# Three seams of a two-part attention kernel: matmuls in pairs, loads and norms moved ahead, a last step in banks of its own

## What is computed

```
x = x + dense_attention(layernorm(x))          # 16 heads of 64, causal penalty -50, softmax over 512
y = layernorm(x)
for i in range(6):
    y = local_attention(shift_tokens(y), Wqkv[i], q_scale[i], k_scale[i], Wo[i]) + y
    #   q, k: divided by their norm per head, times a scale, rotary tables; windows of 32 that
    #   look at themselves and at the window before
    y = ffn(shift_tokens(y), ln_g[i], ln_b[i], W1[i], b1[i], W2[i], b2[i]) + y
    #   layernorm; (a * gelu(gate)) @ W2 + b2, inner width 341
out = x + y
# shift_tokens: of each token the upper 64 channels are those of the token before
```

## Time and profile before

| | us |
|---|---|
| median of 3 runs (lowest to highest) | 2168.26 (2166.22 to 2171.08) |
| the profiled execution: its own time | 2178.13 |
| its span, first to last instruction | 2176.4 |
| PE busy | 2060.6 (95%) |
| DVE busy | 1491.7 (69%) |
| POOL busy | 1451.8 (67%) |
| ACT busy | 1317.8 (61%) |
| DMA queue q1, share of 16 engines | 36.5% |
| mean granted TensorE clock, share of full | 0.976 |

### The profile page before, as it was taken

The page is one execution under the profiler, slowest core; times in us unless marked ns, Lnnn a source line. Parts: engine busy times, 40 slices in busy tenths (PEclk is TensorE's granted clock), DMA queues, the critical chain, the costliest instruction groups (busy, mean ns, idle before and its releaser), DMA issues. The chain is left out here.

```text
span 2176.4 us, 61276 instructions
## 1 busy us (share of the span) xinstructions
PE 2060.6 (95%) x23760; PEld 1286.0 (59%) x23760; DVE 1491.7 (69%) x3292; ACT 1317.8 (61%) x2522; POOL 1451.8 (67%) x1438
## 2 busy tenths in 40 slices
PE   8999999997589999999999999999999999999984
PEld 4555554553356566666666666666666666666652
DVE  5555565553677677777777777787777777777741
ACT  5666656654255566665666666666666666666651
POOL 3334443332677788888877888787887788778740
PEclk9999999998699999999999999999999999999996
DMA  2000000002245555455554564545544455444520
GB/s 64 6 1 6 1 1 6 1 1 71 75 109 132 131 138 127 106 131 148 133 126 104 133 169 111 126 112 134 158 118 118 116 148 142 117 117 122 125 60 22
DMA packets 217695, 204.95 MB, mean 94 GB/s; under 512 B 31682, under 2 KB 210880, under 8 KB 217408
## 3 DMA queue, kind: packets, MB, share of 16 engines
q1 hardware_dynamic: 217408, 201.04, 36.5%
HBM read 83.53 MB, written 13.63 MB: 45 GB/s over the span
## 5 line engine op out<-in xcount | busy, mean ns | idle before, releaser
L736 POOL TENSOR_TENSOR T<-T,RB 128x512 f32<-128x512 f32 x384 | 480.4, 1285 | 237.5 <-DMA RB<-norms 237.5
L684 POOL TENSOR_TENSOR T<-T 128x512 f32<-128x512 f32 x384 | 491.9, 1283 | 58.0 <-DVE T L679 57.6
L658 PE MATMUL bank<-XT,WQK 128*128 128x256 f32 x1536 | 404.2, 397 | 28.4 <-DVE T L679 19.6
L770 PE MATMUL bank<-WU,XT 128*32 128x512 f32 x3072 | 415.5, 601 | 1.5 <-ACT U L777 1.4
L413 POOL TENSOR_SCALAR PR<-PR,RI 128x512 f32<-128x512 f32 x256 | 173.9, 691 | 314.1 <-DVE RI L354 314.1
L664 ACT ACTIVATE SQ<-bank 128x512 f32<-128x512 f32 x384 | 224.6, 599 | 243.2 <-PE bank L658 242.9
L658 PEld LDWEIGHTS bank<-XT,WQK 128*128 128x128 f32 x1536 | 279.5, 194 | 151.2 <-issue 68.4
L678 DVE TENSOR_TENSOR T<-bank,TAB 128x512 f32<-128x512 f32 x384 | 261.9, 682 | 138.0 <-POOL T L684 64.2
L349 DVE CUSTOM_DVE_ANT_0 PR<-bank,causal 128x512 f32<-128x512 f32 x256 | 174.2, 681 | 201.1 <-PE bank L192 201.0
L777 ACT ACTIVATE U<-bank 128x512 f32<-128x512 f32 x384 | 228.7, 596 | 97.0 <-PE bank L770 96.4
L679 DVE TENSOR_TENSOR T<-bank,TAB 128x512 f32<-128x512 f32 x384 | 261.2, 680 | 0.0
(11 more groups left out here) (113 smaller groups left out, 3136.3 us busy)
## 6 DMA issues: line engine op xcount, KB each, us to landing
RB<-norms SPq DMA_DIRECT2D x384, 128.0 KB, 3.4
KZ<-T SPq DMA_DIRECT2D x384, 128.0 KB, 2.5
QP<-T SPq DMA_DIRECT2D x192, 256.0 KB, 4.8
TAB<-rotary_dram SPq DMA_DIRECT2D x24, 512.0 KB, 5.6
norms<-RN SPq DMA_DIRECT2D x96, 128.0 KB, 1.7
WQK<-wqk_halves_dram SPq DMA_DIRECT2D x12, 512.0 KB, 5.8
WVS<-wv_turned_dram SPq DMA_DIRECT2D x29, 128.0 KB, 3.4
WOS<-wo_lanes_dram SPq DMA_DIRECT2D x29, 128.0 KB, 3.6
```

Source lines behind the costliest of these rows:

```text
L658: m = pe.matmul(b[:, ab * HALF:(ab + 1) * HALF], WQK[n % 3][:, i, ab, :], XT[s % 2][:, hf * HALF:(hf + 1) * HALF], start=True, stop=True)
L684: pool.tensor_tensor(t1, t1, T2[i % 2][:, ::-1, :], ALU.add).then_inc(l_rotated.sem, 1)
L736: pool.tensor_tensor(t1, t1, RB[:, i:i + 1, :].to_broadcast([P, 2, HALF]), ALU.mult).then_inc(l_scaled.sem, 1)
L770: i = pe.matmul(bank[1][h * WIN:(h + 1) * WIN, :], XT[s % 2][:, c0:c0 + WIN], WU[:, lp * HG + h, :], start=True, stop=True)
```

## The change

There are four edits; the rest of both parts stays, instruction for instruction.

The core of the diff (left out: ACT's and DVE's new dense orders, which follow PE's, and the early norm's helpers, which are the old ones with other semaphores):

```diff
+        def load_first():
+            sp.dma_start(QSC[:, :], qsc).then_inc(s_i, 16)
+            for n in range(2):
+                load_weights(n)
+            for part in range(4):
+                load_table(part)
...
             def pe_project_q(u):
...
+                if u >= 2:
+                    pe.wait_ge(s_kkept, u + 1)
+                pe.matmul(bank[7 if u >= 2 else 6][:, :], W0[:, 0, p * P:(p + 1) * P], XNT[:, b * SEQ:(b + 1) * SEQ], start=True, stop=True).then_inc(s_q, 1)
...
             def pe_dense_program():
                 pe_ln_turn(0)
-                for g in range(-5, STEPS1 + TPB):
...
+                for h in range(-3, 2 * UNITS + 3):
+                    u, side = divmod(h, 2)
...
+                    if unit(u):
+                        pe_turn(2 * h)
...
+                    if side == 0 and unit(u + 1):
+                        pe_project_v(u + 1)
+                    if side == 1 and unit(u + 2) and not (vo or ln):
+                        pe_project_k(u + 2)
+                    if unit(u):
+                        pe_turn(2 * h + 1)
+                    if side == 0 and unit(u - 2) and u < UNITS:
+                        pe_project_out(u - 2)
...
+                    if unit(u - 1) and u != UNITS - 1:
+                        pe_values(u - 1, 2 * side)
+                        pe_values(u - 1, 2 * side + 1)
...
+                    if h != -2 and unit((h + 2) // 2):
+                        pe_scores(2 * h + 4)
+                        pe_scores(2 * h + 5)
...
+                    if g >= 90 and g % 4 == 2 and (g - 90) // 4 < 4:
...
+                        fold_scale(0, (g - 90) // 4).then_inc(s_fold, 1)
...
-                sp.dma_start(X2S[1:P, :, DH:E], xb[0:P - 1, :, DH:E]).then_inc(s_shift, 16)
+                for r0, r1 in ((0, 112), (112, P - 1)):
+                    sp.dma_start(X2S[r0 + 1:r1 + 1, :, DH:E], xb[r0:r1, :, DH:E]).then_inc(s_shift, 16)
...
+            def up_bank(s, i):
+                return bank[6] if s < LAST else bank[(0, 2, 3, 5, 1, 4)[i]]
...
+            def pe_last_down():
...
+                for c, (c0, n) in enumerate(FFR):
+                    pe.wait_ge(f_gated.sem, f_gated.at(LAST, c))
+                    for t in range(TPB):
+                        i = pe.matmul(bank[6][:, t * E:(t + 1) * E], GE[c][0:n, t * P:(t + 1) * P], W2S[0:n, c, :], start=c + t == 0, stop=c == len(FFR) - 1, skip_group_check=True)
+                i.then_inc(f_down_done.sem, 1)
...
             def act_layers_program():
                 act.preload_act_table_set('natural_log_exp_and_others')
-                for b in range(BATCH):
-                    r = slice(b * TPB, (b + 1) * TPB)
-                    act.activation(XM[:, r, :], X[:, r, :], ACT.Copy).then_inc(lxm.sem, 1)
+                r = slice((BATCH - 1) * TPB, BATCH * TPB)
+                act.activation(XM[:, r, :], X[:, r, :], ACT.Copy).then_inc(lxm.sem, 1)
...
             def pool_layers_program():
-                pool_ln2(0)
                 pool.wait_ge(s_i, 16 * NI)
-                for part in range(4):
-                    pool_fold_scale(0, part)
+                pool.sem_inc(l_folded.sem, 4)
                 for k in range(-8, TOTAL + 3):
                     pool_slot(k)
+                pool_ffn_norm(LAST)
                 pool_ffn_b2(LAST - 1)
-                pool_ffn_norm(LAST)
-                pool_ffn_b2(LAST)
+                pool_last_rest()
```

More of the change, by code:

```diff
@@ L87, in build @@
         s_k = keep.enter_context(nc.semaphore('s_k'))
+        HALF = SEQ // 2
+        WQK = [sb(f'WQK{i}', [P, HG, 2, P]) for i in range(3)]
+        TAB = sb('TAB', [P, 2, 2, 2, SEQ])
+        QSC = sb('QSC', [P, DEPTH * 4])
+        B1T = sb('B1T', [P, DEPTH * 6])
+        B2A = sb('B2A', [P, DEPTH, E])
+        GBA = sb('GBA', [P, 2, DEPTH])
+        s_i = keep.enter_context(nc.semaphore('s_i'))
+        s_wk = [keep.enter_context(nc.semaphore(f's_wk{i}')) for i in range(3)]
+        s_tb = [keep.enter_context(nc.semaphore(f's_tb{i}')) for i in range(4)]
+        NI = 5
         UNITS = BATCH * PAIRS
@@ L160, in pe_project_q @@
                 if u == 0:
[L161 to L167, removed]
                     pe.wait_ge(s_wqkv[1], 16)
-                if u >= 3:
-                    pe.wait_ge(s_res, u - 2)
+                if u >= 4:
+                    pe.wait_ge(s_res, u - 3)
                 else:
                     pe.wait_ge(s_vkept, u)
+                if (u - 2) % PAIRS == 3:
+                    pe.wait_ge(s_vok, u // PAIRS + 1)
+                if u % PAIRS == 7 and u < UNITS - 1:
+                    pe.wait_ge(s_xnt, b + 2)
                 pe.matmul(bank[7][:, :], W0[:, 1, p * P:(p + 1) * P], XNT[:, b * SEQ:(b + 1) * SEQ], start=True, stop=True).then_inc(s_kd, 1)
@@ new lines, in act_dense_program @@
+                for h in range(-3, 2 * UNITS + 3):
+                    u, side = divmod(h, 2)
+                    ahead = unit((h + 1) // 2)
+                    if ahead:
+                        act_exp(2 * h + 2, 0)
+                        act_exp(2 * h + 2, 1)
+                    if unit(u):
+                        act_keep_probs(2 * h)
+                    if side == 0 and unit(u + 1):
+                        act_keep_v(u + 1)
+                    if side == 1 and unit(u) and u % PAIRS == 3:
+                        act_first_vo(u // PAIRS)
+                    if side == 1 and 0 <= u < UNITS - PAIRS and u % PAIRS == 5:
+                        act_ln_keep(u // PAIRS + 1)
+                    if ahead:
+                        act_exp(2 * h + 3, 0)
+                    if unit(u):
+                        act_keep_probs(2 * h + 1)
+                    if ahead:
+                        act_exp(2 * h + 3, 1)
+                    if side == 0 and PAIRS <= u < UNITS and u % PAIRS == 4:
+                        act_early_keep(u // PAIRS - 1)
+                    if side == 1 and unit(u + 2):
+                        act_keep_q(u + 2)
+                    if side == 1 and unit(u - 1) and u != UNITS - 1:
+                        act_keep_values(u - 1)
+                    if h == 2 * UNITS - 2:
+                        act_keep_values(u - 1)
@@ L537, in build @@
             s_shift = ctx.enter_context(nc.semaphore('s_shift'))
-            NI = 5
             sigs = []
@@ L1305, in sp_layers_program @@
                 sp_shift(LAST)
+                for b in range(BATCH):
+                    sp_out(b)
+                sp.wait_ge(s_d, 16 * BATCH)
                 for i in range(3):
```

360 lines of the change are left out of this document (194 added, 166 removed).

## The result

Before and after ran side by side. The kernel after took 2103.39 us (median of 4 runs, 2099.16 to 2106.78), the kernel before 2169.67 us (4 runs, 2166.22 to 2172.57): a ratio of 0.9685, 95% interval 0.9667 to 0.9704. A later comparison on another chip gave 0.9666 (0.9653 to 0.9679). So the change takes 66 to 73 us off; the prediction was 71.5, to 2096.8 us.

A forecast was written before the change was run, and what follows sets the result against it. PE bounds the dense part; a loop through POOL, SP and DMA paces the layers. Terms -22 - 17 - 11 - 21.5 = -71.5 us from the 2168.3 median give 2096.8, own range 2083 to 2110, with rivals 2079 to 2119.

The forecast's parts named there:

- loop scale, relayout, RB: Layers: this loop through POOL, SP and DMA sets the pace, with PE having under 2% of slack.
- Edit 1: Dense part: paired score and value groups on PE save 0.74 us per unit; -22 us, bounds -24 to -12.
- the price of the projections: Dense part: projections cost 0.95 ahead of values and 0.89 ahead of a turn, saving about 0.10 us per unit for two.
- the part's end: End of the dense part: values and projection of the second last unit come later, 0.9 us set against edit 1.
- The rival that the copies of bank 7 hold PE up: Dense part: late ACT or bank 7 copies leave half units as long as before; edit 1 gives 0, 2119; chance 0.11.
- Edit 2: Seam: loads, folds and early norms moved into the dense part; -17 us, bounds -12 to -20.
- Edit 3: Shift split into 112 and 15 rows spreads over DMA engines: -11 us in the layers, -6 at the end.
- the term for the layers: Layers, edit 3: blocked issues ending after the scale go, 11.9 us together, taken as -11; bounds 0 to 20.7 and some.
- PE is the floor: Layers, rival: PE's own time caps the loop's gain, edit 3 gives 3 instead of 11, 2105; chance 0.10.
- Edit 4 with the end: Last step: six products back to back, with the shift's 6 us and some clock gain; -21.5 us, bounds -13 to -26.5.
- The 7.3 us of the working: Last step: full clock instead of half would save 7.3 us on products and down chunk; 2.2 was taken.

The follow-up runs named there:

- split_only: The kernel before with only the shift of 127 rows split into DMAs of 112 and 15 rows; 0.9941 of before, -12.8 us.
- proj_last: The kernel after with projections Q and out behind the values of their half unit instead of ahead, in PE's order; 0.9692 of before.
- unsplit: The kernel after with the shift in one DMA of 127 rows again; 0.9723 of before.
- after_again: The kernel after, unchanged, measured once more beside three other variants; 2101.96 us, 0.9666 of before.
- warm_end: The kernel after with ten products without use around the last step's turn, nine ahead and one behind; 0.9676 of before.
- rb_first: The kernel after with the next front's RB loads issued on SP ahead of the relayout instead of behind it; 2218.27 us, 1.0199 of before.
- pairs_only: The kernel before with only the dense programs of after, without early norms, loads and folds in them; 0.9934 of before, -14.3 us.

## Why the prediction was right, and where it was not

**The reading of the bound** held for the dense part: PE sets the pace and DVE, ACT and POOL follow, but for the four short waits told above. For the layers it held in part. The loop scale, relayout, RB is still the chain's main part, and the prediction had it as what sets the pace; but what it cost was the 20.5 us in 1300 that PE stood idle, and with 5.9 us left PE is as good as the floor.

**Edit 1: the mechanism right, the size off, -14.3 measured for -22.** The step that failed is the price of the projections: 0.95 for Q and 0.99 or less for out. Both take 1.06 in after; turn, V and K came as priced or nearly (0.93 to 0.95, 0.89, 0.86), and so did the pairs (1.87 and 1.92). The unit shown saves 0.52 instead of 0.74.

The rest of the working came out right only in sum. Over the 28 units from the first residual to the 29th, before takes 445.1 us and after 433.1: 12.0 saved, 0.43 a unit, where 0.74 makes 20.7. Units that carry other work save from 0.98 down to less than nothing. The three units that are left were put at 2.2 less the 0.9 for the part's end, 1.3 saved. Measured, beside split_only, the start loses 3.5 us (50.90 against 47.37), which the prediction did not have, and the last three units gain 5.0 (26.3 against 31.3), where it saw a loss. That 1.5 is near 1.3 is luck.

The rival that the copies of bank 7 hold PE up would have explained 1.06; proj_last speaks against it. Why a projection takes 0.86 in one place and 1.06 in another stays open. The earlier trace rows had 0.95 for a projection ahead of values and 1.06 for a single score group, and a dearer price for Q and out should have been one of the bounds.

**Edit 2: right.** -17 forecast, 18.7 in the profiles, 12.0 and 7.6 us for its halves by undoing them. The order of what comes late next (turn, front, product, norms, RB, scale) was as written: product 6.4 us behind the boundary for 6, scale 21.5 us behind it, under the 28.

**Edit 3: the split spreads, but the term for the layers was too large.** The end is as priced (-6.3 in the profiles of before and after; 5.0 with the split alone, 7.0 with it undone). In the layers I took the whole lateness of 11.9 us that I had found. With the split alone about 8 us went; with it undone in after, 1 to 5 came back. A relayout that leaves late isn't late for the scores by as much: unsplit has 9.4 us of such lateness and a stretch only 4 to 6 us longer. This is what the rival "PE is the floor" said, with its 3 us instead of 11; for this term it was nearer than my forecast.

**Edit 4 with the end: right.** -23.6 for -21.5, and 12.1 of it are the banks. The 2 us above the forecast are the clock's: of the gain between half and full clock the working took 2.2 us, which leaves 9.4 for the six products, and they took 7.47 (8.15 in after_again). warm_end shows 5.4 when PE stays busy. The rest of the chain came as counted: 7.45 us from the statistics to the first product for 7.05, and 6.2 behind the products for 6.4. The 7.3 us of the working is itself off: with the 0.95 per product that it names the sum is 6.8.

**The sum.** 14.3 + 19.6 + (1 to 8) + 23.6 is 58.5 to 65.5 us. Measured are 66 and 73. The forecast of 71.5 so has errors of -7.7 (edit 1) and 3 to 10 (edit 3) that the end and edit 2 make up by 2 to 3 us each and something in the layers by the rest. That the sum came within 7 us of the measured time is in good part luck.

That something is time in which PE waits. The stretch of the layers was 1478 to 1488 us in the three profiles of kernels with the old seam and end, with or without the split, and 1466 to 1472 in the profiles with the new seam or one half of it (rb_first aside). PE's idle time from 700 to 2000 us goes with it: 20.5 us in before, 15.0 in pairs_only, 13.9 in split_only, 12.6 in unsplit, and 5.2 to 7.9 in the nine others (73.9 in rb_first). Part of the 1488 of before is the clock: it fell twice in the layers, behind waits of PE of 1.90 and 3.36 us, which happened in no other profile but that of rb_first. By the granted clock of these rows (columns as in the earlier trace rows) that cost at most 25 x 0.07 + 25 x 0.14 = 5 us, an estimate.

```profile
650.00:675.00 25.00, 22.41 (x328) 14.69 (x327) 17.69 (x34) 12.70 (x25) 18.64 (x16) 0.93 0.56 133
...
750.00:775.00 25.00, 21.64 (x246) 13.88 (x249) 13.76 (x26) 13.30 (x26) 19.03 (x21) 0.86 0.64 169
```

Why PE still waits 6 to 9 us longer in split_only than in the kernels with the new seam is not settled. By the medians what is left over is 0.5 to 14.5 us, with an interval of 3 to 4 us on each term. Buffers that lie elsewhere in memory since tables and weights were moved are one candidate; it wasn't tried.

## What to carry to other kernels

Price a regrouping on the bound engine by the dearest neighbour that its groups have in the trace, not by the mean: the same projection cost 0.86 to 1.06 us by its place. Cut a DMA whose row count is prime into parts that divide well, and look first where its landing or the queue behind it is on the path, since in the layers held-up issues of 1.6 us cost nothing and at the end each microsecond counted. Where lateness in a queue is summed up from rows, take it as an upper bound, compare it with the idle time of the engine that is nearest to full, and subtract two profiles only after looking at how each stands to its median and where two profiles of the same code differ.

## What the runs showed of the hardware

- The shift of 127 rows of 1 KB (4 pieces of 256 B each) took 9.2 us to the statistics at a DMA share of 0.08, 53 and 74 rows together 6.8 at 0.11, 64 and 63 rows 3.1 at 0.31, 112 and 15 rows 2.9 at 0.53. That 53 and 74 took more than half of 127 would fit if 53 rows and half of the 74 went through the same engine (90 rows, and 90/127 of 9.18 is 6.5; an estimate from these rows, not shown).
- A shift in one DMA, at a share of about one engine, held up a later issue on the same queue: the norms' issue behind it took 3.0 to 5.3 us instead of 0.34 in before, 2.3 to 5.7 in unsplit. Behind 53 and 74 rows it took 1.1 to 2.0.
- Ten products without use kept the granted clock at 1.00 through the last step, where 4.7 us of idle PE had it at 0.50 until the third product: 5.41 against 7.47 and 8.15 us for the same six.
- A projection of 128x512 took 0.86 us between two turns, 0.95 between a turn and single values, and 1.05 to 1.06 us between a turn or values and a pair of scores or values.
- Executions of the same dense order ended their first unit 2 us apart (50.7 to 50.9 us in five profiles, 52.8 to 53.5 in six), and kept that distance to the end of the part.
